# First attention: values and logits of two tiles a step in one joint product of 136 columns

## The reference, cut to what matters

```python
xn = _layernorm(x, axis=-1)                      # x: (4, 1024, 256)
q = (hidden_states @ Wq.T + bq)                  # hidden_states is xn; 256 columns
k = (hidden_states @ Wk.T + bk)                  # 128 columns
v = (hidden_states @ Wv.T + bv)                  # 128 columns
# rotation, normalisation, random projection, sin/cos features of q and k, then
kv = jnp.einsum('bhsf,bhsd->bsfd', kp, v)
out = jnp.einsum('bhsf,bsfd->bhsd', qp, kv)
...
logits = xt @ wg.T                               # router of the first experts: 8 columns of xn
```

## Time and profile before

| | |
|---|---|
| median of 3 runs | 1881.21 us |
| lowest, highest | 1877.51, 1885.34 us |
| the profiled execution's own time (its span) | 1883.0 us |
| mean granted TensorE clock | 0.928 |
| TensorE busy | 1653.7 us (88%) |
| VectorE busy | 1371.1 us (73%) |
| ScalarE busy | 1035.7 us (55%) |
| GpSimd busy | 669.0 us (36%) |
| first attention | from 0 to about 358 us of the span |

### The profile page before, as it was taken

One profiled execution on the slowest core, in us unless ns is written; L12 is line 12 of the kernel. 1 busy time (PEld: TensorE's weight loads), 2 busy tenths in 40 slices (PEclk: granted clock), 3 DMA queues, 4 the chain that ended last, 5 costly groups with the idle time before them and its releaser, 6 DMA issues. The chain is left out here.

```text
span 1883.0 us, 34976 instructions
## 1 busy us (share of the span) xinstructions
PE 1653.7 (88%) x9842; PEld 1290.4 (69%) x9842; DVE 1371.1 (73%) x3710; ACT 1035.7 (55%) x2473; POOL 669.0 (36%) x842
## 2 busy tenths in 40 slices
PE   6999798579992676999999999997889999988997
PEld 5988686469992554545455555543789999967775
DVE  6487999546666886999988888852656666657777
ACT  2345466236664673366666666665556666643443
POOL 2444488530005653022126767630000000056662
PEclk8678899899996797799999999998999999999999
DMA  9313346654443789224245555414964444445552
GB/s 345 116 34 72 80 127 168 164 184 132 134 127 116 232 301 295 60 69 103 61 97 147 155 153 161 148 32 128 269 200 133 132 132 130 126 155 168 160 169 79
DMA packets 291880, 272.73 MB, mean 145 GB/s; under 512 B 138153, under 2 KB 260714, under 8 KB 289644
## 3 DMA queue, kind: packets, MB, share of 16 engines
q1 hardware_dynamic: 267960, 215.41, 39.3%
q0 software_dynamic: 18432, 50.36, 8.8%
q10 hardware_dynamic: 5332, 4.96, 0.8%
HBM read 136.84 MB, written 133.69 MB: 144 GB/s over the span
## 5 line engine op out<-in xcount | busy, mean ns | idle before, releaser
L1876 ACT ACTIVATE ca_PT<-ca_psS 128x512 f32<-128x512 f32 (+3 forms) x768 | 335.8, 495 | 205.0 <-PE ca_psS L1913 200.6
L1417 POOL DMA_INDIRECT g_y<-ys_scratch,pos x128 | 125.2, 978 | 433.9 <-POOLq L73 363.0
L1792 DVE CUSTOM_DVE_ANT_0 ca_masked_row<-ca_psM,mask_row 128x384 f32<-128x384 f32 (+3 forms) x512 | 224.2, 486 | 45.9 <-PE ca_psM L1896 43.9
L1913 PE MATMUL ca_psS<-ca_QS,ca_KS 128*128 128x512 f32 (+1 forms) x480 | 174.9, 368 | 1.7 <-ACT ca_PT L1876 1.6
L1796 DVE TENSOR_REDUCE ca_part<-ca_psM 128x1 f32<-128x512 f32 x256 | 163.4, 684 | 16.0 <-PE ca_psM L1896 14.6
L1925 PE MATMUL ca_psO<-ca_PT,ca_VA 128*17 128x512 f32 (+3 forms) x1536 | 161.0, 491 | 6.1 <-ACT ca_OT L1868 6.1
L1896 PE MATMUL ca_psM<-ca_KS,ca_QS 126*128 126x512 f32 (+2 forms) x480 | 157.9, 376 | 7.3 <-DVE ca_part L1792 5.0
L790 PE MATMUL fa_psO<-fa_weighed,ident 128*128 128x256 f32 x512 | 133.5, 420 | 26.0 <-DVE fa_weighed L584 26.0
L1913 PEld LDWEIGHTS ca_psS<-ca_QS,ca_KS 128*128 128x128 f32 x480 | 90.2, 189 | 87.9 <-ACT ca_PT L1876 59.6
L391 POOL DMA_INDIRECT xs_scratch<-x_sb,pos x128 | 124.6, 973 | 55.9 <-ACT ca_PT L1876 34.1
L991 PE MATMUL f_psU<-ffn_lo,f_x_hi 128*128 x428 | 139.4, 326 | 0.0
(11 more groups left out here) (271 smaller groups left out, 4801.5 us busy)
## 6 DMA issues: line engine op xcount, KB each, us to landing
xs_scratch<-fa_blank SPq DMA_DIRECT2D x32, 640.0 KB, 4.9
x_sb<-xs_scratch SPq DMA_DIRECT2D x143, 128.0 KB, 2.1
ys_scratch<-x_sb SPq DMA_DIRECT2D x143, 128.0 KB, 1.7
xs_scratch<-fa_blank SPq DMA_DIRECT2D x32, 384.0 KB, 6.6
spare<-qk_scratch SPq DMA_DIRECT2D x24, 512.0 KB, 7.4
ca_QS<-qk_scratch SPq DMA_DIRECT2D x20, 512.0 KB, 6.6
ca_KS<-qk_scratch SPq DMA_DIRECT2D x20, 512.0 KB, 8.0
x_sb<-in_ffn SPq DMA_DIRECT2D x16, 608.0 KB, 4.1
```

Source lines behind the costliest of these rows:

```text
L1417: pool.indirect_dma_start(y[:, t % R, k, :], None, y_dram, bass.IndirectOffsetOnAxis(pos[:, t, k:k + 1], 0)).then_inc(got[t % R], 16)
L1792: ins = dve.tensor_tensor_reduce(masked_row[:, (n * NU + u) % BANKS, h * w:(h + 1) * w], bank[:, h * w:(h + 1) * w], mask_row[:, CHUNK - w ...
L1876: act.activation(PT[:, s % PTS, h, off:CHUNK], psS[(GH * s + h) % BANKS][:, off:CHUNK], ACT.Exp)\
L1913: pe.matmul(psS[tile % BANKS][:, off:CHUNK], KS[slot][:, h, kt * P:(kt + 1) * P], QS[slot][:, h, c * CHUNK + off:(c + 1) * CHUNK], start=T ...
```

## The change

The value block and the logit products of one tile become one block with a moving operand of 136 columns (128 + 8, `NVE`). It is made for two tiles in a step, in steps 2 to 17, so all 32 tiles are done by step 17 and steps 18 to 33 hold no value block. ScalarE copies values of two tiles at once (256 columns) and logits of two tiles (16 columns) one step later than before, ahead of `take_qkv`; `take_v` and `keep_logits` are gone.

```diff
+    NVE = NV + E0
...
             def weigh(t, i, b):
                 dve.wait_ge(centred, t + 1)
-                dve.wait_ge(v_out, t + 1)
+                dve.wait_ge(v_out, t // PAIR + 1 if isinstance(t, int) else PAIRS)
...
             def high_half(q):
                 act.wait_ge(xT_done, q + 1)
                 if PAIR * q >= RING:
-                    act.wait_ge(v_done, PAIR * (q + 1) - RING)
+                    act.wait_ge(qk_done, PAIR * (q + 1) - RING)
...
-            def keep_logits(t, i, b):
-                if isinstance(t, int) and t < PAIRS:
-                    act.wait_ge(v_done, t + 1)
-                    act.activation(logits[:, PAIR * t:PAIR * (t + 1), :], psV[:, NV:NV + PAIR * E0].rearrange("p (t e) -> p t e", e=E0),
-                                   ACT.Copy).then_inc(logits_out, 1)
+            def take_values_and_logits(q):
+                act.wait_ge(v_done, q + 1)
+                two, both = slice(PAIR * q, PAIR * (q + 1)), psV[:, 0:PAIR * NVE].rearrange("p (t n) -> p t n", n=NVE)
+                act.activation(v[:, two, :], both[:, :, 0:NV], ACT.Copy).then_inc(v_out, 1)
+                act.activation(logits[:, two, :], both[:, :, NV:NVE], ACT.Copy).then_inc(logits_out, 1)
...
-            def take_v(t, i, b):
-                act.wait_ge(v_done, t + 1)
-                act.activation(tile_of(v, t), psV[:, 0:NV], ACT.Copy).then_inc(v_out, 1)
...
                 if 0 <= n - 1 < PAIRS:
                     high_half(n - 1)
+                if 0 <= n - 3 < PAIRS:
+                    take_values_and_logits(n - 3)
                 if n == min(ROUTED):
                     routing.exponentials(act)
...
-            in_steps(act, (2, take_qkv), (10, sines), (2, take_v), (2, keep_logits), (3, keep_rotT), (13, take_out), (10, squares), (4, keep_p),
+            in_steps(act, (2, take_qkv), (10, sines), (3, keep_rotT), (13, take_out), (10, squares), (4, keep_p),
...
-                if t >= 1:
-                    pe.wait_ge(v_out, t)
-                    pe.wait_ge(logits_out, min(t, PAIRS))
-                three_passes(pe, psV[:, 0:NV], lambda k: x_hi(t, k), lambda k: x_lo(t, k), lambda k: w_all[0][:, k, NQK:NQK + NV],
-                             lambda k: w_all[1][:, k, NQK:NQK + NV], KT, last=False, check=True)
-                ins = pe.matmul(psV[:, 0:NV], ones[:], b_two[:, NQK:NQK + NV], start=False, stop=True, skip_group_check=True)
-                if t < PAIRS:
-                    for j, s in enumerate(range(PAIR * t, PAIR * (t + 1))):
-                        ins = three_passes(pe, psV[:, NV + j * E0:NV + (j + 1) * E0], lambda k: x_hi(s, k), lambda k: x_lo(s, k),
-                                           lambda k: w_all[0][:, k, NQK + NV:], lambda k: w_all[1][:, k, NQK + NV:], KT, check=True)
+
+            def values_and_logits(q):
+                pe.wait_ge(lo_done, q + 1)
+                if q >= 1:
+                    pe.wait_ge(v_out, q)
+                    pe.wait_ge(logits_out, q)
+                for j, t in enumerate(range(PAIR * q, PAIR * (q + 1))):
+                    out = psV[:, j * NVE:(j + 1) * NVE]
+                    three_passes(pe, out, lambda k: x_hi(t, k), lambda k: x_lo(t, k), lambda k: w_all[0][:, k, NQK:W0],
+                                 lambda k: w_all[1][:, k, NQK:W0], KT, last=False, check=True)
+                    ins = pe.matmul(out, ones[:], b_two[:, NQK:W0], start=False, stop=True, skip_group_check=True)
                 ins.then_inc(v_done, 1)
...
-                for lag, stage in ((2, project), (3, transpose_rotated), (12, sum_groups), (4, random_projection)):
+                if 2 <= n < TILES + 2:
+                    project(n - 2, (n - 2) % POS_TILES, (n - 2) // POS_TILES)
+                if 0 <= n - 2 < PAIRS:
+                    values_and_logits(n - 2)
+                for lag, stage in ((3, transpose_rotated), (12, sum_groups), (4, random_projection)):
```

## The result

The changed kernel took 1863.39 us (median of 4 runs, 1849.78 to 1867.35) against 1880.93 us for the kernel before (4 runs): ratio 0.9891, 95% interval 0.9861 to 0.9920. 1855 was forecast; the gain is 17.5 us in the first set and 24.6 in the second, against 26.

What follows compares the result with a forecast made beforehand. TensorE was taken to bound steps 2 to 17 and VectorE the rest of the stage. Gains 0.4 + 14.3 + 13.5 - 1.0 = 27.2 us took the profiled 1883.0 to 1855.8, stated as 1855, range 1840 to 1876.

Steps and rivals of the forecast that it cites:

- What bounds the stage: First attention: TensorE, often at half clock, bounds 18.87 to 169.66 us (steps 2 to 17); VectorE bounds 169.66 to 352.
- the first rival: Clock stays as it is in steps 2 to 17, only fewer products pay: about 8.8 us gained, 1872; chance 0.16.
- Price of a joint block: TensorE, steps 2 to 17: a 136-column block costs 1.88 us at 0.50 and 1.08 at 1.00, two 3.76 and 2.16.
- The rival of dear columns: 136-column blocks in steps 2 to 17 cost more, 16 us given back, 1871; chance 0.06.
- Steps 2 and 3: Both at the slow clock, 13.9 us after against 14.3 before: gain 0.4 us.
- Steps 4 to 11: Clock 1.00 in 70% of steps 5 to 10: 55.3 us after against 69.6 before, gain 14.3 us.
- Steps 12 to 17: TensorE and VectorE close, 8.9 us a step: 53.4 us after against 66.9 before, gain 13.5 us.
- Steps 18 to 33: 17.1 us of value blocks leave TensorE, worth nothing since VectorE is the limit there.
- The rival of a lost clock: Steps 18 to 33 lose TensorE's clock through longer waits: 42 us in 16 steps at 0.55, 1897; chance 0.08.
- The new wait for the copies: TensorE's joint block waits for ScalarE's copies: 0.3 us a step taken, inside the 6.3 us a step, up to 1.59.
- The routing: Last copy of logits moves to the head of step 18, so VectorE waits: about 1 us lost, bounds 0 and 4.
- All of it reaches the end: VectorE's bound stretch begins earlier and is otherwise the same, so all 27.2 us come off 1883.0, giving 1855.8.

Runs made afterwards that it cites:

- wide_logits: The kernel before with only the logit products of steps 2 to 17 widened from 8 to 136 columns, the extra values unused: 1863.88 us, ratio 0.9909.
- idle_blocks_late: The changed kernel with an unused value block of 128 columns put back in each of steps 18 to 33: 1863.02 us, ratio 0.9913.
- moved_apart: The changed kernel with values of two tiles a step in 128 columns and logits apart again in products of 8 columns: 1912.08 us, ratio 1.0162.
- joint_again: The changed kernel unaltered, measured again with 6 runs: 1855.55 us, ratio 0.9852.
- tiles_ahead: The changed kernel with VectorE's normalise one step ahead and its low half behind the weighing: 1849.90 us, ratio 0.9826.
- copies_later: The kernel before with only ScalarE's copies of values and logits one step later, at the head of the step: 1888.01 us, ratio 1.0040.
- ahead_not_joined: The kernel before, values and logits apart, with VectorE's normalise one step ahead and its low half behind the weighing: 1876.22 us, ratio 0.9989.
- ahead_spread: The changed kernel with normalise one step ahead, low half and inverse of norms behind the weighing, dependent operations parted: 1866.94 us, ratio 0.9955.

## Why the prediction was right, point by point

- **What bounds the stage.** Right, and shown. The first half was TensorE's by its clock (`wide_logits`), the second VectorE's (`idle_blocks_late`, by the length of its stretch). The Trainium skill (TensorE: Matmul & The Clock Gate, Part 1) ties the clock to sustained activity against idle stretches; the page alone would have given 1872, the first rival, and a TensorE that idled 1.9 of 78.1 us was slow again in `moved_apart` (0.65).
- **Price of a joint block.** Right: 2.15 us for two against 2.16. The rival of dear columns is out. The working of one price in it is wrong: 12 x 1.07/1.87 x 0.215 is 1.48 us for the logit products of a fast step, not 1.36. The trace before has 1.36 (step 3, 31.43 to 32.79 us), so the number was right and its source wasn't; only the first rival's 0.27 us a step used it.
- **Steps 2 and 3.** A gain of 0.4 us was said, and step 4 began 1.2 us later (34.7 against 33.5): all of steps 2 and 3 ran slow now, where half of step 3 had been fast before, and the working left out step 3's rotated transposes (0.70 us) and one of the two transposes of tiles (0.77): 15.4 us were measured, not 13.9. The clock of 1.00 that the earlier trace rows give for this stretch can't be right for all of it: the q/k block of step 2 lasts 2.81 us in both kernels (19.64 to 22.45 in the one before), the price at 0.50.
- **Steps 4 to 11.** 55.3 us were said, 52.1 and 50.5 measured in two executions; the clock taken, 0.7 x 1.00 + 0.3 x 0.50 = 0.85, was 0.88 and 0.89. The sum is right in part by errors that cancel: step 4 took 6.6 us and not 9.2, steps 5 to 10 took 34.4 and not 37.8, and step 11, put at 8.3, took 11.1, with the wait for the normalised tiles in it.
- **Steps 12 to 17.** 53.4 us were said. 54.7 in `joint_again`, 61.7 in the first profile. This is the term that was mis-sized in the first set: steps 13 to 15 took 8.6, 8.6 and 8.5 as worked out (8.54), but steps 12, 16 and 17 took 13.8, 11.0 and 11.3. "Waits between them come to some tenths" left out two waits that the trace before had shown, the one for the norm every fourth step (15.2 us in the earlier trace rows) and the one for VectorE's first heavy step (1.89 us ahead of step 12). In the first profile TensorE waited 4.62 us ahead of step 12 and 1.47 us ahead of step 17, in `joint_again` 3.27 and nothing. The full clock, which 8.54 us a step takes for granted, was not there in step 12 (0.58) and step 17 (0.70) of the first profile. Why it fell ahead of step 12 stays open, since it did so before that wait began.
- **Steps 18 to 33.** Worth nothing, as said (189.4 against 188.4 us). The rival of a lost clock did not come: the clock sank from 0.95 to 0.93 and TensorE had the slack; VectorE was busy 95% of the stretch.
- **The new wait for the copies.** Up to 0.3 us a step was taken; TensorE waited 1.8 us for them in all (0.71 in step 11, 1.09 in step 16).
- **The routing.** A loss of 1 us with bounds 0 and 4: against the kernel before, the lead at the start of the weighing fell from 22.9 us (step 17) to 19.7 (step 18) in the first profile, and from 28.3 to 28.2 in `joint_again`. A term that varies within its bounds.
- **All of it reaches the end.** Nearly: from the last copy of this stage to the end the kernel before took 1524.9 us, the changed one 1527.7 and 1526.3.

The sum for the first profile is -1.2 + 17.9 + 4.5 - 1.0 - 2.8 = 17.4 us (1883.0 - 1865.6); for `joint_again` -1.3 + 19.5 + 11.5 - 1.0 - 1.4 = 27.3 us, where 27.2 had been worked out. That closeness is partly luck, since the two executions of one kernel are 10 us apart; the range was the better statement.

## What to carry to other kernels

When TensorE is busy without a gap and still slow, set the granted clock beside the order of time and look for products with few columns: joining them with wider ones, or even widening them and throwing the rest away, can pay more than leaving them out. Once the clock is up, a short wait can cost more than itself: behind the same 1.09 us in step 16 the clock fell in `joint_again` (11.0 us) and held in `tiles_ahead` (9.3). So look next for the steps in which another engine is late. Where executions of one kernel lie 10 us apart, set several of them, and the clock of each, beside a single profile. An order that takes a wait from one stretch has to be read in all the stretches that share it.

## What the runs showed of the hardware that was not expected

- 128 wasted columns in each of 192 products made the kernel 17 us faster (`wide_logits`, 1863.88 against 1881.37).
- Products of 8, 128 and 136 columns take the same time from start to start inside a block: about 0.215 us at 0.50, about 0.11 at 1.00 (products of 384 columns: 0.32 and 0.175).
- The clock fell with TensorE busy throughout in the joined kernel too (40.2 us), and ahead of a long wait and not behind it (78.1 us in `joint_again`, the wait from 81.31).
- With the thin products in place the clock's mean from step 4 to step 17 was 0.69, 0.78 and 0.80 in the profiles of the kernel before, `copies_later` and `ahead_not_joined`.
- The same binary gave 13.8 and 9.9 us for the same step, by when the clock came back (98 and 88 us), with waits of 4.62 and 3.27 us ahead of it.
- VectorE's operations of 0.34 and 1.21 us stretched to 1.14 and 2.89 us in places, each time beside a GpSimd tensor_tensor (25 of 25 in `joint_again`, 43 of 43 in `ahead_spread`).
